# The tail of the last layer's context attention and the self-attention behind it, as one stage

## The reference, cut to what matters

```python
# step 4: x = x + _L1_xattn_ref(ctx, _layernorm(x), mask, ...)   16 heads of 64
    out = jnp.einsum('bhij,bhjd->bhid', attn, v)      # attn: softmax over the 2048 + 128 keys
    out = out.transpose(0, 2, 1, 3).reshape(b, m, INNER)          # INNER = 1024
    ...                                               # out @ Wout, layer norm with ln_o_g, ln_o_b
# step 5: x = x + _L1_attn_ref(_layernorm(x), W_qkv, b_qkv)      16 heads of 32
    qkv = x @ W_qkv.T + b_qkv
    q, k, v = (qkv[:, :, 0], qkv[:, :, 1], qkv[:, :, 2])
    q = _rope(q)                                      # pairs (x0, x1) -> (x0 cos - x1 sin, x0 sin + x1 cos)
    k = _rope(k)
    scores = jnp.einsum('bhqd,bhkd->bhqk', q, k) / math.sqrt(D)
    w = jax.nn.softmax(scores, axis=-1)
    out = jnp.einsum('bhqk,bhkd->bhqd', w, v)
# step 6: x = x + _L1_ffn_ref(_layernorm(x), w1, b1, w2, b2)
```

## Time and profile before

| | us |
|---|---|
| median of 3 executions (2146.20 to 2150.58) | 2146.72 |
| profiled execution, its own time | 2148.47 |
| its span, first to last instruction | 2146.7 |

### The profile page before, as it was taken

How to read it: one execution, slowest core, us unless ns; L and a number is a source line. 1 busy time by engine, 2 the same in 40 slices (tenths; PEclk the granted TensorE clock), 3 DMA queues, 4 the chain that set the end, 5 groups by cost and what they waited for, 6 DMA issues and landing times. The chain is left out here.

```text
span 2146.7 us, 44080 instructions
## 1 busy us (share of the span) xinstructions
PE 1958.7 (91%) x17806; PEld 1083.0 (50%) x17806; DVE 1584.1 (74%) x2795; ACT 1030.7 (48%) x1454; POOL 652.2 (30%) x687
## 2 busy tenths in 40 slices
PE   6799999999589879999999999999999999667898
PEld 2455555555445433555555555555555555433643
DVE  5689999999757764777777777777777776545676
ACT  2689998998713632333333333333333343201453
POOL 3244454454312410223333333332333332122000
PEclk9899999999699889999999999999999999988899
DMA  4323332331242210000000000000000000120400
GB/s 148 99 65 85 99 76 75 99 87 46 57 171 81 79 40 22 22 22 23 22 23 23 22 4 20 22 23 22 22 23 23 22 2 2 50 74 0 152 11 20
DMA packets 40138, 106.16 MB, mean 49 GB/s; under 512 B 19328, under 2 KB 21632, under 8 KB 33792
## 3 DMA queue, kind: packets, MB, share of 16 engines
q1 hardware_dynamic: 39936, 103.35, 15.7%
HBM read 75.42 MB, written 1.05 MB: 36 GB/s over the span
## 5 line engine op out<-in xcount | busy, mean ns | idle before, releaser
L1469 POOL TENSOR_SCALAR a1c_p_hi<-a1c_pf 128x512 f16<-128x512 f32 x272 | 201.4, 741 | 665.1 <-ACT a1c_pf L1525 622.7
L1331 PE MATMUL PS<-a_x_hi,w_next 128*128 128x512 f16 x1088 | 280.1, 380 | 6.0 <-POOL a1c_v_lo L1459 3.6
L1341 PE MATMUL PS<-w_next,a_x_hi 128*128 128x512 f16 x1088 | 279.1, 379 | 0.0
L1494 ACT ACTIVATE a1c_k_hi<-PS 128x512 f16<-128x512 f32 x136 | 81.2, 597 | 326.9 <-PE PS L1331 326.9
L392 POOL TENSOR_SCALAR a0c_p_hi<-a0c_r 128x1024 f16<-128x1024 f32 x128 | 154.9, 1210 | 268.6 <-DVE a0c_r L492 265.7
L1501 ACT ACTIVATE a1c_v_hi<-PS 128x512 f16<-128x512 f32 x136 | 81.5, 599 | 259.0 <-PE PS L1341 206.2
L497 DVE TENSOR_TENSOR a0c_p_lo<-a0c_r,a0c_p_hi 128x1024 f16<-128x1024 f32 x128 | 201.6, 1575 | 0.9 <-POOL a0c_p_hi L392 0.9
L1674 DVE TENSOR_TENSOR a1c_p_lo<-a1c_pf,a1c_p_hi 128x512 f16<-128x512 f32 x272 | 198.1, 730 | 5.2 <-POOL a1c_p_hi L1469 5.2
L1525 ACT ACTIVATE a1c_pf<-PS,a_maskc 128x512 f32<-128x512 f32 x256 | 174.9, 685 | 47.9 <-PE PS L1836 38.3
L1617 DVE CUSTOM_DVE_ANT_0 a1c_junk<-PS,a1c_maskr 128x512 bf16<-128x512 f32 x256 | 175.7, 686 | 18.8 <-DVE a1c_ctop L1617 0.5
L492 DVE TENSOR_TENSOR a0c_r<-PS,a0c_r 128x1024 f32<-128x1024 f32 x128 | 155.3, 1213 | 32.8 <-ACT a0c_r L438 32.6
(11 more groups left out here) (362 smaller groups left out, 4550.2 us busy)
## 6 DMA issues: line engine op xcount, KB each, us to landing
a_cf<-in_ctxT SPq DMA_DIRECT2D x16, 1024.0 KB, 5.2
a0c_ks<-a0c_k_hi SPq DMA_DIRECT2D x128, 128.0 KB, 2.3
a1c_cf<-in_ctx SPq DMA_DIRECT2D x16, 1024.0 KB, 4.8
a0c_ks<-a0c_k_lo SPq DMA_DIRECT2D x64, 128.0 KB, 2.4
f_w<-in_w SPq DMA_DIRECT2D x4, 1024.0 KB, 8.6
f_w<-in_w SPq DMA_DIRECT2D x1, 4096.0 KB, 19.5
s1q_w<-in_L1a_wT SPq DMA_DIRECT2D x3, 1024.0 KB, 7.6
qw_raw<-in_w_gate SPq DMA_DIRECT2D x1, 2816.0 KB, 9.1
```

The source lines that it names most:

```text
L1331: mm = nc.tensor.matmul(out, wk[i][:, k, f * P:(f + 1) * P], (x_hi, x_lo)[j][e][:, k, :], start=(step == 0), stop=(step == 11))
L1341: mm = nc.tensor.matmul(out, (x_hi, x_lo)[j][e][:, k, t * P:(t + 1) * P], wv[i][:, k, group * BANK:(group + 1) * BANK], start=(step == 0), ...
L1469: nc.gpsimd.tensor_scalar(p_hi[:, v % 4, :], pf[:, v % 2, :], 1.0, 0.0, ALU.mult, ALU.add)\
```

## The change

The end of context_attention_1 and self_attention_1 become one block, latents_tail. L1x_wo and the q and k thirds of L1a_wT are loaded at the end of the context loop into g.next, as float32 over the float16 pairs, once the last product with them is done; the loop's block waits for them. TensorE goes batch by batch: transposes of a batch and its product, four times; then transposes of z and the three projections of a batch, the transposes of the batch before's rotated q and k behind them; then the attention's steps. ScalarE makes nearly all copies out of PSUM, the key copies among them, and loads the tables for the root and exp by operations on a single column. VectorE does both layer norms for one batch at a time. The sum of the attention's output into x goes from VectorE to GpSimd, which also clears kd at the block's start. In transposes of a batch's features four 128x128 tiles share a bank, and one copy of 128x512 takes them out.

```diff
-def transpose_rows(nc, g, name, src, dst, tiles):
...
-        m_ = Memory(nc, ctx, "a1")
+        acc = Memory(nc, ctx, "a1").sb("acc", [P, B, H, W])
+        weights_in = Memory(nc, ctx, "a1").sem("weights_in")
+        wo, wqk = [g.next[:, 2 * i:2 * i + 2, :].rearrange("p i n -> p (i n)").bitcast(F32) for i in range(2)]
+        wo, wqk = wo.rearrange("p (k n) -> p k n", k=FT), wqk.rearrange("p (k n) -> p k n", k=KT)
+        loop = ctx.enter_context(ExitStack())
+        m_ = Memory(nc, loop, "a1")
         q_hi, q_lo = m_.sb("q_hi", [P, B, FT, P], F16), m_.sb("q_lo", [P, B, FT, P], F16)
-        acc, top = m_.sb("acc", [P, B, H, W]), m_.sb("top", [P, B, H])
...
+                    sp.wait_ge(v_product, 8 * NJ)
+                    sp.dma_start(wo, d["L1x_wo"].rearrange("p (k n) -> p k n", k=FT)).then_inc(weights_in, 16)
+                    sp.dma_start(wqk, d["L1a_wT"].rearrange("p (k n) -> p k n", k=KT)[:, :, 0:2 * D]).then_inc(weights_in, 16)
+                    sp.wait_ge(weights_in, 32)
...
-        with ExitStack() as sub:
-            s = Memory(nc, sub, "a1o")
...
+        loop.close()
+        latents_tail(nc, g, d, acc, wo, wqk, weights_in)
...
-def self_attention_1(nc, g, d):
...
+def latents_tail(nc, g, d, acc, wo, wqk, weights_in):
+    RING = (5, 6, 7, 0, 1, 2)
+    SCORES, TURNS, OUTS = (5, 6, 7), (3, 4), (0, 1, 2)
...
+        p, pT = a[:, 0:2, :].rearrange("p b (i n) -> p (b i) n", i=2), a[:, 2:4, :].rearrange("p b (i n) -> p (b i) n", i=2)
+        qT, y = aT[:, 0:KT, :], aT[:, KT:2 * KT, :].rearrange("p k (i n) -> p (k i) n", i=2)
...
+            @block.sync
...
+                sp.dma_start(bo[:], d["L1x_bo"].broadcast_to([P, D])).then_inc(rows_in, 16)
+                sp.dma_start(go[:], d["L1x_go"].broadcast_to([P, D])).then_inc(rows_in, 16)
+                sp.dma_start(bias[:], d["L1a_b"].broadcast_to([P, 3 * D])).then_inc(rows_in, 16)
+                sp.dma_start(cs[:], d["cos"]).then_inc(rows_in, 16)
+                sp.dma_start(sn[:], d["sin"]).then_inc(rows_in, 16)
+                sp.dma_start(wv[:], d["L1a_wT"].rearrange("p (k n) -> p k n", k=KT)[:, :, 2 * D:3 * D]).then_inc(wv_in, 16)
+            @block.gpsimd
+            def _(pool):
+                nc.gpsimd.memset(warm[:], 0.0).then_inc(warmed, 1)
+                nc.gpsimd.memset(v[:, :, :, W - 1:W], 1.0).then_inc(ones_set, 1)
+                nc.gpsimd.memset(kd[:], 0.0).then_inc(cleared, 1)
+                pool.wait_ge(rows_in, 80)
+                for b in range(B):
+                    pool.wait_ge(based, 3 * b + 2)
+                    rotate(pool, nc.gpsimd, 1, b, k_parts, k_rot)
+                for i in range(2 * B):
+                    b, cols = i // 2, slice(256 * (i % 2), 256 * (i % 2) + 256)
+                    pool.wait_ge(x_done, b + 1)
+                    pool.wait_ge(y_done, i + 1)
+                    nc.gpsimd.tensor_tensor(g.x[:, b, cols], g.x[:, b, cols], y[:, i, :], ALU.add).then_inc(final, 1)
+            @block.tensor
+            def _(pe):
+                def turn_a(b):
+                    pe.wait_ge(a_done, b + 1)
+                    if b >= 1:
+                        pe.wait_ge(aT_done, 2 * b)
+                    for half in range(2):
+                        for k in range(KT):
+                            f = KT * half + k
+                            t = nc.tensor.transpose(g.PS[:, half, k * P:(k + 1) * P], a[:, b, f * P:(f + 1) * P], g.ident[:])
+                        t.then_inc(a_turned, 1)
+                def out_product(b):
+                    pe.wait_ge(aT_done, 2 * (b + 1))
+                    if b == 0:
+                        pe.wait_ge(weights_in, 16)
+                    if b >= 2:
+                        pe.wait_ge(o_done, b - 1)
+                    for k in range(FT):
+                        mm = nc.tensor.matmul(g.PS[:, 3 + b % 2, :], aT[:, k, tokens(b)], wo[:, k, :],
+                                              start=(k == 0), stop=(k == FT - 1))
+                    mm.then_inc(product, 1)
+                def turn_z(b):
+                    pe.wait_ge(z_done, b + 1)
+                    if b >= 2:
+                        pe.wait_ge(based, 3 * (b - 1))
+                    for k in range(KT):
+                        t = nc.tensor.transpose(g.PS[:, RING[(3 * b + 2) % 6], k * P:(k + 1) * P],
+                                                z[:, b % 2, k * P:(k + 1) * P], g.ident[:])
+                    t.then_inc(z_turned, 1)
+                def project(b):
+                    pe.wait_ge(zT_done, b + 1)
+                    for i in range(3):
+                        n = 3 * b + i
+                        if n == 0:
+                            pe.wait_ge(weights_in, 32)
+                        if n == 2:
+                            pe.wait_ge(wv_in, 16)
+                        if n >= 6:
+                            pe.wait_ge(based, n - 5)
+                        for k in range(KT):
+                            right = wv[:, k, :] if i == 2 else wqk[:, k, i * D:(i + 1) * D]
+                            mm = nc.tensor.matmul(g.PS[:, RING[n % 6], :], zT[:, k, tokens(b)], right,
+                                                  start=(k == 0), stop=(k == KT - 1))
+                        mm.then_inc(projected, 1)
+                def turn_rotated(b):
+                    if b == 0:
+                        pe.wait_ge(o_done, B)
+                    for i in range(2):
+                        pe.wait_ge((q_rot, k_rot)[i], 2 * (b + 1))
+                        if b >= 1:
+                            pe.wait_ge((q_out, k_out)[i], (b, HG * b)[i])
+                        for f in range(KT):
+                            t = nc.tensor.transpose(g.PS[:, 3 + i, f * P:(f + 1) * P],
+                                                    rot[:, i, b % 2, f * P:(f + 1) * P], g.ident[:])
+                        t.then_inc((q_turned, k_turned)[i], 1)
...
+                def turn_p(n):
+                    pe.wait_ge(exp_done, n + 1)
+                    if n == 0:
+                        pe.wait_ge(q_out, B)
+                    elif n == 1:
+                        pe.wait_ge(k_out, HG * B)
+                    else:
+                        pe.wait_ge(p_copied, n - 1)
...
+                for b in range(B):
+                    turn_a(b)
+                    out_product(b)
+                for b in range(B):
+                    turn_z(b)
+                    project(b)
+                    if b >= 1:
+                        turn_rotated(b - 1)
+                score(0)
+                score(1)
+                turn_rotated(B - 1)
+                for n in range(2, N + 4):
+                    if n < N:
+                        score(n)
+                    if n < N + 2:
+                        turn_p(n - 2)
+                    if n >= 4:
+                        output(n - 4)
+            @block.scalar
+            def _(act):
+                def copy_a(b):
+                    for half in range(2):
+                        act.wait_ge(a_turned, 2 * b + half + 1)
+                        nc.scalar.copy(aT[:, KT * half:KT * half + KT, tokens(b)],
+                                       g.PS[:, half, :].rearrange("p (k n) -> p k n", k=KT)).then_inc(aT_done, 1)
+                def copy_o(b):
+                    act.wait_ge(product, b + 1)
+                    nc.scalar.copy(o[:, b, :], g.PS[:, 3 + b % 2, :]).then_inc(o_done, 1)
+                def roots(b):
+                    act.wait_ge(ovar_done, b + 1)
+                    nc.scalar.activation(ostd[:, b:b + 1], oveps[:, b:b + 1], ACT.Sqrt).then_inc(ostd_done, 1)
+                    act.wait_ge(xvar_done, b + 1)
+                    nc.scalar.activation(xstd[:, b:b + 1], xveps[:, b:b + 1], ACT.Sqrt).then_inc(xstd_done, 1)
...
+                def copy_rotated(b):
+                    act.wait_ge(q_turned, b + 1)
+                    nc.scalar.activation(qT[:, :, tokens(b)], g.PS[:, 3, :].rearrange("p (k n) -> p k n", k=KT), ACT.Copy,
+                                         scale=DH ** -0.5).then_inc(q_out, 1)
+                    act.wait_ge(k_turned, b + 1)
+                    if b == 0:
+                        act.wait_ge(cleared, 1)
+                    for h in range(HG):
+                        r = slice(h * DH, (h + 1) * DH)
+                        nc.scalar.copy(kd[r, b, :, h * P:(h + 1) * P], g.PS[r, 4, :].rearrange("p (k n) -> p k n", k=KT))\
+                            .then_inc(k_out, 1)
+                act.wait_ge(warmed, 1)
+                nc.scalar.activation(warm[:], warm[:], ACT.Sqrt).then_inc(warmed, 1)
+                copy_a(0)
+                for b in range(B):
+                    copy_o(b)
+                    if b + 1 < B:
+                        copy_a(b + 1)
+                    else:
+                        copy_z(0)
+                    roots(b)
+                act.wait_ge(warmed, 2)
+                nc.scalar.activation(warm[:], warm[:], ACT.Exp).then_inc(warmed, 1)
```

(39 more changed lines are left out.)

399 lines of the change are left out of this document (149 added, 250 removed).

## The result

Four executions of the changed kernel took 2117.40 to 2121.13 us, median 2120.49; the kernel before, timed beside it, 2147.89. The ratio is 0.9868, 95% interval 0.9851 to 0.9886: 28.4 us less by the ratio, 27.4 by the medians, 1.3%. The forecast was 2115.7 in 2112 to 2124. The profiled execution took 2117.40 with a span of 2114.0.

What follows compares the result with a forecast made beforehand. The stage was taken as bound by the order of its steps, not by an engine. Waiting removed, 33.2 us, less 2.2 for clock falls, gave 31.0 off the 2146.72 median: 2115.7 us, range 2112 to 2124.

Steps and rivals of the forecast that it cites:

- Division and product: Stage start: product begins 7.3 us earlier but ends at 1890.9 against 1890.8, eaten by half-clock passes and exposed copies.
- Layer norms: Between product and projections: 5.5 us chain per batch fits under the next batch's 8.8; projections start 22.5 us earlier.
- rival (c): Layer norms: ScalarE, held in the roots, copies products late; gain 21.4 us, time 2125.3; chance 0.07.
- Projections: Four batches of 10.3 us each, now with waits for z of 1.3, 3.9 and 3.9 us; end at 1942.6.
- Turn to attention and attention: After the projections: first output 9.9 us later instead of 28.2, then 30.9 us to the last sum, 30.6 before.
- Fetch: Weights loaded at the context loop's end: landed by 1849.6, before the block's end; uncovered, at most 3 us of start.
- GpSimd's clearing: Memset of kd, 6.9 us beside the divisions: costs them 0, at worst 6.2 us.
- rival (b): Stage start: the clearing of kd holds back the divisions by 6.2 us; gain 24.8, time 2121.9; chance 0.05.
- Clock: TensorE's waits in the stage: about 1.5 falls to half clock at 1.5 us each, 2.2 us; between 0 and 7.5.
- Rival (a): Half clock at every TensorE wait (7.5 us), ScalarE's key copies 0.72 each; gain 23, time 2123.7; chance 0.12.
- Rival (d): Product and projections: TensorE stays at half clock, slower; with two thirds at half clock 2164.5 us; chance 0.02.

Runs made afterwards that it cites:

- e_a_mid: The changed kernel with the next batch's a transposed in the middle of this batch's product with L1x_wo, copies before the product's own; 2116.4 us, ratio 0.9833.
- e_norms_first: The changed kernel with the layer norms' overlap undone: TensorE waits for z of all four batches before transposing the first; 2128.8 us, ratio 0.9910.
- e_scores_last: The changed kernel with the overlap at the turn undone: batch 3's rotated q and k transposed and copied before the first score; 2123.6 us, ratio 0.9875.
- e_no_ahead: The changed kernel with the fetch ahead undone: L1x_wo and L1a_wT's q and k thirds loaded in the new stage; 2122.6 us, ratio 0.9868.
- e_same: The changed kernel run and profiled once more, unchanged; 2120.5 us, ratio 0.9861, stage 133.8 us.
- e_best: e_all plus batch 2's rotated q and k transposes and the first two scores ahead of batch 3's v product; 2109.4 us, ratio 0.9819.
- e_turn: e_best with VectorE's maxima and subtractions of scores 0 and 1 before v's bias, and 8 identity transposes in the first wait; 2105.2 us, ratio 0.9789.
- e_all: The changed kernel with the next a transposed mid-product, the next z inside the projection ahead, batch 0's z in the last product; 2105.6 us, ratio 0.9799.
- e_best_busy: e_best with 24 identity transposes into an unused bank while TensorE waits for the first division; 2106.7 us, ratio 0.9805.

## Why the prediction was right

Set beside the prediction's schedule, with its times shifted by the 2.6 us by which the stage starts earlier in the first profile:

| step | predicted | shifted | measured |
|---|---|---|---|
| first product's end | 1864.6 | 1862.0 | 1862.4 |
| last product's end | 1890.9 | 1888.3 | 1888.8 |
| first projection | 1892.3 | 1889.7 | 1890.17 |
| end of batch 0 | 1902.6 | 1900.0 | 1900.6 |
| end of batch 1 | 1914.2 | 1911.6 | 1912.2 |
| end of batch 2 | 1928.4 | 1925.8 | 1929.9 |
| V (end of batch 3) | 1942.6 | 1940.0 | 1944.4 |
| V to first output | 9.9 | | 10.1 |
| first output to last sum | 30.9 | | 31.0 |

- *Division and product*: right, 0.4 us late. The half-clock passes cost 2.2 us (9.31 against 7.13), 1.7 assumed. That the earlier start brings nothing by itself held: exposed copies of 1.9 us a batch (transposes among them) ate it, and e_a_mid takes 2.9 us of them out. (A transpose at full clock is 0.104 us by the row that the prediction names, not 0.107; measured are 0.109, eight in the 0.87 us from 1912.25 to 1913.12.)
- *Layer norms*: right. Done one batch at a time they lie under the product, and e_norms_first prices it: 12.7 us with the clock. The chain of a batch, 6.5 us from the product's end to z (5.7 of them on VectorE, 5.5 forecast), never held ScalarE: its second root is done at 1868.23 and it then waits 3.2 us for the next product, so rival (c) is refuted.
- *Projections*: waits of 1.3 and 4.2 where 1.3 and 3.9 stood. The key copies took 0.59 each, just over the assumed 0.49 to 0.58. The prediction missed a wait: normalising batch 3 needs z's buffer back from batch 1's transposes and so sat on VectorE from 1895.1 to 1901.28:

```profile
1894.98 0.16 DVE L2187 RECIPROCAL lt_xrstd<-lt_xstd 128x1 f32<-128x1 f32 x1 [0.27 <-ACT lt_xstd L2104]
1901.28 0.55 DVE L2191 TENSOR_SCALAR lt_z<-g_x,lt_xmv,lt_xrstd 128x512 f32<-128x512 f32 x1 [6.14 <-PE PS L1994]
```

  This held back the bias and rotation of batch 0 behind it, so that k was rotated at 1910.6, 1.6 us before TensorE needed it. It cost nothing here, and that is luck: the forecast did not count with it.
- *Turn to attention and attention*: 28.2 to 10.1 us, and 31.0: right. e_scores_last gives 4.7 us to the overlap, about 3.4 of them without the clock.
- *Fetch*: hidden; the later load, issued at 1828.07, landed by 1841.4, 7 us before the stage begins (issue, size, us to landing):

```profile
w_next<-in_L1a_wT SPq DMA_DIRECT2D x1, 2048.0 KB, 13.3
```

  But the prediction priced its absence at most 3 us, and e_no_ahead measured 3.6 at the first product. And it said that the fetch ahead does nothing, because L1x_wo was hidden already: so it was behind the divisions of all four batches, not in an order that starts the first product behind one. The forecast is the same either way, since it has the fetch ahead.
- *GpSimd's clearing*: rival (b) is refuted by one row. The divisions beside the memset take 4.63 us as before:

```profile
1848.99 6.95 POOL L1952 MEMSET lt_kd<- 128x8192 f32 x1
...
1849.50 4.63 DVE L2154 TENSOR_TENSOR lt_a<-a_acc,lt_rec 128x1024 f32<-128x1024 f32 x4
```

  The Trainium skill (SBUF — State Buffer, Who interferes with whom) expected this, and the row agrees.
- *Clock*: the term that was mis-sized, and the one with no fixed size. 2.2 us were allowed; the first profile has one fall of 3.06 and some tenths in the attention, e_same no fall in the projections. Hence stage gains of 28.4 and 31.2 around the forecast's 31.0. That e_same comes within 0.2 us is luck in part: it spent hardly any of the 2.2, and 2.0 us of small overruns took their place (0.4 up to the last product's end, 0.8 more in the projections' waits and passes, 0.2 in the turn, 0.45 in the attention). Rival (a), a fall at every wait, is refuted: no wait of 0.7 to 0.8 us in the stage began one, and those of 2.7 us did in 3 of 14. The evidence against it was read too early, though: the loop's last 24 us at 1.00 end at 1849.30, and in the same trace the clock is at 0.50 from 1850.0 on, behind a wait of TensorE of 1.49 us:

```profile
1849.30:1850.00 0.70, 0.58 (x14) 0.99 0.00 0
1850.00:1851.20 1.20, 0.74 (x12) 0.50 0.00 0
```

  (The kernel before: length, TensorE's busy time, granted clock, DMA share, GB/s.) Rival (d) is refuted by a granted clock of 1.00 from 1862.5 to 1916.3.

The median lies 4.8 us above the forecast. 1.2 of it is the kernel before, whose median was 2147.9 beside it and 2146.7 ahead of it. The first profile's stage is 2.65 longer than the forecast's 134.0, e_same's 0.2 shorter; which of the two the executions without a trace resemble stays open, as does the rest, which is no more than what the stretches outside the stage vary by.

Where the 31.2 us come from, by stretches of the two traces (before against e_same):

| stretch | before | e_same | change |
|---|---|---|---|
| first reciprocal to last product's end | 39.3 | 39.8 | +0.5 |
| to the first projection | 24.0 | 1.3 | -22.6 |
| to V | 43.0 | 51.2 | +8.2 |
| to the first output product | 28.2 | 10.1 | -18.1 |
| to the last sum | 30.6 | 31.35 | +0.8 |

The waits before the projections and before the attention go, and a fifth of that comes back inside the projections, where z's and the rotated tiles' transposes and their copies now stand. By the runs that undo one part: fetch ahead 3.6, norms under the product 6.6 without clock, overlap at the turn about 3.4 without clock. These 13.6, if they add up, leave 17.6 for what no run undid by itself: block ends and barriers, the norms' order step by step over four batches, and the key copies spread over batches. How these share it is not shown.

## What to carry to other kernels

When stages of different engines are merged, walk each engine's list once more: the waits that stayed (4.2 us before zT, 1.9 between batches, 3.1 in e_best) went, in whole or in part, by a new order of TensorE's, ScalarE's or VectorE's list alone, and moving z's transposes and copy ahead of those of q and k (6.0 us) was worth more than the fetch ahead (3.6). Put the small transposes and copies that open the next step into the middle of the present long product: of the 13.4 us between e_same and e_turn 11.2 came with e_all, 6.0 of which z's place ahead of the rotated tiles brings alone. And judge an edit of a few us by the length of its stage in the trace, since stretches that it does not touch moved by up to 6 us.

## What the runs showed of the hardware beside this

- Equal waits of TensorE need not have equal consequences: of 14 waits of 2.7 us, 3 were followed by 1.7 to 3.1 us of loss at half clock. Of two waits at the same place, 3.06 us in e_best and 3.07 in e_best_busy, only the second was followed by a fall. The one of 6.4 us was, with 2.45 us lost in the passes and 0.5 around the transposes before them. No wait of 0.7 to 0.8 us in the stage began a fall. The Trainium skill (TensorE: Matmul & The Clock Gate, What's actually happening) says of a kernel's start that the number of slow matmuls of one kernel differs from run to run with the gate's phase; e_same against the first profile (7.13 against 10.19 us for the same 16 passes) shows such a difference in the middle of a kernel.
- A clock that is down at the start of a stage need not be that stage's doing: in e_best_busy it was 0.99 between 1849 and 1850 and 0.50 from there on, with TensorE idle 1.49 us shortly before (1847.8 to 1849.3). In nine of the fourteen traces the fall came later, in the wait for the first division or within 0.2 us of its end. Where it came early, 8 transposes more at the start (e_turn) bring no earlier rise, and 24 (e_best_busy) do, and cost as much as they bring.
- ScalarE's copies from PSUM with 32 partitions cost no less than those with 128: four of 32x512 take 2.36 us in a row, 0.59 each; one of 128x512 takes 0.59, and two in a row 1.08.
- VectorE and GpSimd slow each other when both do this rotation. From 1906.5 to 1910.9 of the first profile, VectorE's five operations of 128x256 on SBUF beside GpSimd's take 0.64 to 1.06 us, where those from 1902.5 to 1904.7, with GpSimd idle, take 0.42 to 0.43; GpSimd's own four beside them take 0.90 to 1.02, where 0.73 to 0.84 is usual. VectorE's divisions beside GpSimd's memset were not slowed (4.63 us).

```profile
1904.27 0.42 DVE L1933 TENSOR_TENSOR lt_rot<-lt_ta,lt_tb 128x256 f32<-128x256 f32 x1
...
1908.85 1.06 DVE L1928 TENSOR_TENSOR lt_tb<-lt_raw,lt_cs 128x256 f32<-128x256 f32 x1
```
